# Filler matmuls into an unused PSUM bank in eight waits of TensorE, in a two-layer perceiver kernel on one core

## What is computed

```python
x = x + _L0_xattn_ref(_layernorm(x), ctx_2048, seg, ...)   # 16 heads, latent queries/keys, window of 9 keys a query
x = x + _L0_attn_ref(_layernorm(x), ...)                   # gated state-space mixer, 512 channels, 16 states, a scan
x = x + _L0_ffn_ref(_layernorm(x), ...)                    # 256 -> 1024 -> 256, gelu of a rounded value
x = x + _L1_xattn_ref(_layernorm(x), ctx_2048, ...)        # 16 heads of 16, all 4096 context rows, 8-bit rounding
x = x + _L1_attn_ref(_layernorm(x), ...)                   # self-attention over the pair of batches
x = x + _L1_ffn_ref(_layernorm(x), ...)                    # shared expert and routed expert, 256 -> 1152 -> 256
```

## Time and profile before

| | |
|---|---|
| median of 3 runs | 547.14 us (542.32 to 548.55) |
| the profiled execution | 546.76 us |
| its span, first to last instruction | 544.9 us |
| mean granted TensorE clock, by the page | 0.937 |
| busy: TensorE, VectorE, ScalarE, GpSimd | 80%, 73%, 54%, 25% |

### The profile page before, as it was taken

One profiled execution on the slowest core, in us unless ns is written; L12 is line 12 of the kernel. 1 busy time (PEld: TensorE's weight loads), 2 busy tenths in 40 slices (PEclk: granted clock), 3 DMA queues, 4 the chain that ended last, 5 costly groups with the idle time before them and its releaser, 6 DMA issues.

```text
span 544.9 us, 9508 instructions
## 1 busy us (share of the span) xinstructions
PE 437.3 (80%) x3874; PEld 328.4 (60%) x3914; DVE 398.5 (73%) x607; ACT 296.0 (54%) x384; POOL 138.8 (25%) x176
## 2 busy tenths in 40 slices
PE   3999887788488777767866789899898988876597
PEld 3556776666265555533753567677677767654486
DVE  6134585357969999995669899999999999613242
ACT  2123424045454444431437899999999999931110
POOL 4124441013545555550001233242111111100000
PEclk9999996989699999989889799999999999977789
DMA  8820692131122111004519545544455334000000
GB/s 300 344 91 0 195 246 100 37 158 36 43 95 80 60 58 58 2 0 169 217 47 396 203 159 229 226 165 156 174 228 219 157 156 156 2 1 0 1 1 19
DMA packets 14822, 67.94 MB, mean 125 GB/s; under 512 B 6154, under 2 KB 8762, under 8 KB 11706
## 3 DMA queue, kind: packets, MB, share of 16 engines
q1 hardware_dynamic: 14202, 63.78, 31.8%
q0 software_dynamic: 576, 3.54, 1.7%
HBM read 66.16 MB, written 1.15 MB: 124 GB/s over the span
## 4 chain that ended last, share of the span: by engine, by line
PE 54%; DVE 17%; issue 14%; ACT 8%; DMA 3%; POOL 2%; SPq 1%; DVEq 0%; ACTq 0%; POOLq 0%
PE ps L1705 10%; PE ps L1684 6%; PE ps L1718 4%; PE ps L1793 3%; ACT arena L915 3%; PE ps L1717 3%; DVE arena L1138 3%; DVE arena L1147 3%; PE ps L1375 2%; PE ps L1377 2%; PE ps L1395 2%; DVE arena L1100 2%; PE ps L1505 2%; PE ps L1626 2%; PE ps L1573 2%
## 5 line engine op out<-in xcount | busy, mean ns | idle before, releaser
L1245 DVE CUSTOM_DVE_ANT_0 arena<-ps,arena 128x1024 f32<-128x1024 f32 x88 | 109.1, 1279 | 3.7 <-PE ps L1684 3.6
L1705 PE MATMUL ps<-cst,arena 128*128 128x128 f32 x512 | 78.8, 277 | 18.5 <-ACT arena L915 16.8
L1705 PEld LDWEIGHTS ps<-cst,arena 128*128 128x128 f32 x512 | 61.1, 141 | 50.9 <-ACT arena L906 32.5
L906 ACT ACTIVATE arena<-arena 128x4096 uint8<-128x4096 f32 x22 | 81.7, 3714 | 7.1 <-POOL arena L682 7.0
L1684 PE MATMUL ps<-arena 128*128 128x512 bf16 x216 | 68.5, 383 | 8.0 <-DVE arena L1245 3.4
L1718 PE MATMUL ps<-vrow,arena 128*128 128x16 f16 x1024 | 60.5, 169 | 0.0
L1718 PEld LDWEIGHTS ps<-vrow,arena 128*128 128x128 f16 x1024 | 54.1, 97 | 1.4
L1245 DVE CUSTOM_DVE_ANT_0 w<-ps,arena 128x1024 f32<-128x1024 f32 x40 | 50.0, 1279 | 3.6 <-PE ps L1684 2.7
L915 ACT ACTIVATE arena<-ps 128x512 f32<-128x512 f32 x96 | 50.0, 586 | 1.6 <-PE ps L1718 1.5
L1717 PE MATMUL ps<-vrow,arena 128*128 128x16 f16 x768 | 49.9, 170 | 0.0
L649 POOL TENSOR_TENSOR arena<-arena 128x1024 f32<-128x1024 f32 x16 | 37.5, 2366 | 47.6 <-DVE arena L1138 47.3
(11 more groups left out here) (266 smaller groups left out, 818.3 us busy)
## 6 DMA issues: line engine op xcount, KB each, us to landing
arena<-ks_scr SPq DMA_DIRECT2D x16, 2048.0 KB, 8.1
arena<-in_context SPq DMA_DIRECT2D x16, 512.0 KB, 3.4
arena<-in_w SPq DMA_DIRECT2D x1, 4488.0 KB, 13.5
w<-in_w SPq DMA_DIRECT2D x1, 2927.0 KB, 13.6
arena<-in_w0b SPq DMA_DIRECT2D x1, 2560.0 KB, 11.2
arena<-in_w SPq DMA_DIRECT2D x1, 2048.0 KB, 8.3
arena<-bc_scr SPq DMA_DIRECT2D x16, 128.0 KB, 3.5
arena<-in_fill SPq DMA_DIRECT2D x1, 2048.0 KB, 7.0
```

What stands on the lines that cost most here:

```text
L906: act.activation(out8[:, :, 0], s_sb[u % 3], ACT.Exp, bias=nb[:, u % 3:u % 3 + 1], accum_out=zall[:, u:u + 1]).then_inc(p_ready, 1)
L1245: dve.tensor_tensor_reduce(s_sb[slot][:, keys], ps[:, 2 * (c % 2):2 * (c % 2) + 2, :].rearrange("p a n -> p (a n)"), ksb[h % 2][:, keys], ...
L1705: mm = pe.transpose(bank(4 + n % 3, k * P, P), words[:, w:w + P], ident)
```

## The change

A tile `busy` of 512 bf16 values a partition is set to 1.0 by GpSimd. TensorE multiplies it 28 times into bank 3 before it waits for the first weights. A helper `awake(n)` does n matmuls of the bf16 identity against itself, repeated four times, into bank 3: 12 at the head of `columns(1)` to `columns(5)`, 5 before the transposes of the attention output, 14 before the transposes of the self-attention output. TensorE also waits for the bf16 identity (ScalarE writes it at 4.72 us) ahead of the first weights. Nothing reads bank 3's filler.

```diff
--- before.py
+++ after.py
@@ -143,6 +143,7 @@
         early = vrow.rearrange("k p n -> k (p n)").bitcast(F32)
         csums = early[:, 0:B * CT * D].rearrange("k (b t d) -> k b t d", b=B, t=CT)
         w0q = early[:, B * CT * D:B * CT * D + W0Q]
+        busy = early[:, B * CT * D + W0Q:B * CT * D + W0Q + 256].bitcast(BF16)
         w_dq = w0q[:, 0:CH * QC].rearrange("p (c n) -> p c n", c=CH)
         w_kcat = w0q[:, CH * QC:CH * (QC + 2 * R)].rearrange("p (c n) -> p c n", c=CH)
         w_qr = w0q[:, CH * (QC + 2 * R):W0Q].rearrange("p (h n) -> p h n", h=H)
@@ -324,6 +325,7 @@
         hT = take([FT + 1, T])
         assert at[0] <= 2 * KEYS
 
+        busy_set = sem("busy_set")
         pe_step = sem("pe_step")
         (WABS, QLAT, MTR, MLAT, MLA_OUT, DLAT, DBC, DLIN, MIX_OUT, FF_OUT, Q_PS, Q_TR, ON_TR, X_OUT, Q_MADE,
          KEYS_MADE, VALUES_MADE, OA_TR, SA_OUT, LOGITS) = range(1, 21)
@@ -574,6 +576,7 @@
 
         @block.gpsimd
         def _(pool):
+            pool.memset(busy[:, :], 1.0).then_inc(busy_set, 1)
             pool.memset(neghalf[:, :], -0.5).then_inc(half, 1)
             pool.wait_ge(half, 1)
 
@@ -1327,8 +1330,15 @@
 
         @block.tensor
         def _(pe):
+            def awake(n):
+
+                for _ in range(n):
+                    pe.matmul(bank(3, 0, 512), identb[:, :], identb[:, :].unsqueeze(1).broadcast_to([P, 4, P]), start=True, stop=True)
+
             def columns(k):
 
+                if k:
+                    awake(12)
                 pe.wait_ge(ln_rows, 2 * (k + 1))
                 for c in range(CH):
                     for b in range(B):
@@ -1336,7 +1346,11 @@
                 mm.then_inc(ln_tr, 1)
 
 
+            pe.wait_ge(busy_set, 1)
+            for _ in range(28):
+                pe.matmul(bank(3, 0, 512), busy[:, 0:P], busy[:, :], start=True, stop=True)
             pe.wait_ge(ld_cst, 16)
+            pe.wait_ge(identb_ready, 2)
             pe.wait_ge(ld_w0a, 16)
             for h in range(H):
                 pe.matmul(bank(h // 8, (h % 8) * KVC, KVC, 0, QC), w_uqT[:, h, :], w_ukT[:, h, :], start=True, stop=True)
@@ -1737,6 +1751,7 @@
                 weighted(UNITS - 1, c)
 
 
+            awake(5)
             pe.wait_ge(on_rows, 1)
             for c in range(CH):
                 for b in range(B):
@@ -1764,6 +1779,7 @@
             projected(1, 1, 1).then_inc(pe_step, 1)
             projected(0, 2, 5)
             projected(1, 2, 6).then_inc(pe_step, 1)
+            awake(14)
             pe.wait_ge(oa_rows, B)
             for c in range(CH):
                 for b in range(B):
```

## The result

The changed kernel takes 527.81 us (median of four executions: 523.34, 526.63, 528.98 and 538.56), against 547.8 (four, 542.32 to 548.55). The ratio is 0.963 (0.953 to 0.973). The profiled execution is the one of 523.34 (span 521.5), 23.4 us less than the one profiled before.

What follows compares the result with a forecast made beforehand. TensorE at the lower clock (1.2 of 2.4 GHz) in the first 46 us and behind idle gaps was the bound. Savings 15.7 + 4.45 + 2.25 + 2.6 + 4.1 = 29.1, less 3, give 547.14 - 26.1 = 521.0 us; range 512 to 537.

Steps and rivals of the forecast that it cites:

- start, to the first L1409: From launch through the query rounds: 28 fillers raise the clock early, saving 2.4 + 0.95 + 12.75 - 0.4 = 15.7 us.
- gaps 1, 2, 3: First three layer-norm waits: 12 fillers each keep the clock up for work behind; 4.45 us together, the third trimmed for a transfer.
- five before the attention output: Five fillers in a 1.24 us gap: save 2.25 if they hold the clock, delay by 0.9 if it has fallen.
- gap 4 and the 14: Layer-norm wait and self-attention output: faster matmuls, but filler becomes the late one by 0.5; 2.6 us saved.
- gap 5: Last layer-norm wait: the transposes, L1785 and L1793 behind it run at the high clock; 4.1 us saved.
- allowance for falls: 3 us taken off the sum, since fillers cover only 2.6 of 3.6 to 4.1 us and some gaps fall anyway.
- The reading of the first stretch: First 46 us: the strip's 1.00 is absence of a record; durations show TensorE at the lower clock level.
- They cost 0 to 1.2; I take 0.4: Delay of L1342 by the 28 start fillers, ending at 8.8 to 10.3 us against its start at 9.10.
- Everything to 105.87 hangs on this chain, so it moves along: Work behind the query rounds keeps the start's full 15.7 us; 8 if a transfer of the context were late.
- Rival B: Clock rises but falls back in the first query rounds, 96 rows wide and behind two ScalarE-copy waits: 533.8 us, chance 0.2.
- Rival C: Fillers do not hold: remaining idle drops the clock at every gap, and the start falls back too: 543 us, chance 0.08.
- Rival D: Slower: the clock does not rise on matmuls of one constant bf16 tile, all fillers cost 0.43: 563 us, chance 0.04.

Runs made afterwards that it cites:

- bridged: Changed kernel plus three filler bridges in the start (34 instead of 28 fillers, 6 and 2 more at the ScalarE-copy waits): 522.55 us, ratio 0.958.
- w3b_later: Changed kernel with the load of the last weights (w3b) issued behind the second head's key scales instead of before them: 538.35 us, ratio 0.978.
- the fourth experiment: Same run as w3b_later: changed kernel with the w3b load moved behind the second head's key scales; 538.35 us, ratio 0.978.
- the bridged start: Kernel before plus start fillers only, 34 before the first weights, 6 and 2 at the waits for ScalarE's copies, none in later gaps: 533.97 us, ratio 0.979.
- The version without any low stretch: Changed kernel with bridged start, 16 instead of 12 fillers in layer-norm gaps, and fillers in every other long TensorE wait: 513.9 us, ratio 0.943.

## Why the prediction was right, and where its steps were off

The forecast was 26.1 us less; the medians give 20.0 less, the profiled executions 23.4. The predicted 521.0 is 6.8 us under the measured median; the profiled execution, 523.34, is 2.3 above it, and the executions reach from 520.8 to 540. The forecast was the fast heap of a kernel that has several. Step by step, on the profiled executions (the measured column adds up to 23.4):

| place | predicted | measured |
|---|---|---|
| start, to the first L1409 | 15.7 | 14.5 |
| from there to 105.87 | 0 | -2.5 |
| gaps 1, 2, 3 | 1.6, 1.55, 1.3 | 1.6, 1.5, 1.5 |
| attention loop: behind its tenth product, at its end | 0, 0 | -0.4, -1.1 |
| five before the attention output | 2.25 | 1.4 |
| gap 4 and the 14 | 2.6 | 2.7 |
| gap 5 | 4.1 | 4.1 |
| allowance for falls | -3 | 0 |

The closeness to the profiled execution is in part luck. Without the allowance the sum was 29.1; the 3 were taken off for falls at the gaps, which did not come in this execution, and stood in for other losses: 1.2 in the start, 2.5 behind it, 1.5 in the loop.

*The reading of the first stretch was right*, and it was most of the gain. The page's 1.00 there was no reading: L1389 went from 2.08 to 1.13. The rounds gave 12.5 (from 17.82 to the copy at 36.04 is 18.2, against 30.7), for 12.75 predicted; L1356 came out at the estimated 2.9.

*"They cost 0 to 1.2; I take 0.4" was mis-sized, for a reason that was not the fillers.* L1356 began 1.7 us later than L1342 did, since the weights landed later; the kernels without fillers in the start show the same (10.56, 11.03). A landing time from one profiled execution was taken for a constant. That is the 1.2 missing in the start.

*"Everything to 105.87 hangs on this chain, so it moves along" failed by 2.5.* The chain does move along to 49.38, 14.5 earlier. Then its DMA store takes 3.97 instead of 2.89, and GpSimd's sum 3.43 instead of 2.35: 1.1 each, and L1436 (the old L1422) waits for both. Behind them the clock is low over 66.80 to 80.50, 13.7 us instead of the 10.3 of before, for half a microsecond more. Whether the store and the sum are longer because they now fall into busier stretches was not tried.

*"If the clock has already fallen, they take 2.15 and delay by 0.9" is what happened* at the attention output: the five took 2.29, and delayed L1758 by about 0.7. The case was written down and not chosen. What they gave all the same is L1763 at 1.99 instead of 3.78: a late filler that runs at the lower level can still pay, since the work behind it ran at the higher.

*The transfer was named for gap 3 ("a transfer of scales also holds VectorE") and 0.2 was taken off for it.* Gap 3 brought 1.5 at the first L1248, and the wait for the scales grew from 0.90 to 2.39, but that is not where the loop lost: by the tenth product it was level (13.42 against 13.43). The loop lost its 1.5 elsewhere, and no term had that: *"The attention loop between 306 and 475 is paced by VectorE and gets no filler; I leave it as it is"*. TensorE is on its chain at both ends, and the clock decides how long that takes. At the end the clock falls earlier than before: the reciprocal begins 4.9 to 5.0 us behind the loop's last eviction in the five profiled executions with fillers at the gaps and none in the loop, 3.95 to 3.96 in the four without fillers at the gaps, and 3.96 again in the three with fillers at the loop's end too. Why fillers elsewhere bring that fall about is open.

*"From this I take 3" was about right for some executions, and did not cover the larger risk.* In the execution of 523.34 not one of the five gaps fell, with 1.0 to 1.5 us idle and a copy behind each; in those of 523.57 (bridged) and 539.99 gaps 1 and 2 did, for 3.2 us. The larger risk lay in the start, which I had at full value, and there it is over ten microseconds in single executions and nothing in others. Of eleven executions of the change nine lie from 520.8 to 529.7 and two at 538.6 and 540.0.

*Rival B* had half of the right reason, and a time, 533.8, that no execution of the change took (w3b_later's 533.69 is its slow start and the longer loop together). "Ahead of them are two waits for ScalarE copies" is the cause, as the profile of the fourth experiment and the bridged start show; "the 96-row rounds never raised the clock" is true (27.7 against 46.4) but does not make it fall: in the changed kernel four rounds run without its transposes (L1377), from 17.82 to 26.16, at full rate. A third place, the wait for the first weights, was in no case of mine.

*Rival C* fell as a whole; what it said of the gaps happened at two of five in two profiled executions. The rule beside it, in the Trainium skill, "TensorE: Matmul & The Clock Gate", Part 1, that the ramp costs under 1% of a typical span, doesn't hold for this kernel: the start alone, bridged, is worth 2.1%. The version without any low stretch is 5.7% faster than the kernel before.

*Rival D* fell with the first row: 28 fillers in 8.23 us.

## What to carry to other kernels

Read TensorE's clock from the duration of one repeated instruction, not from the strip, above all ahead of the first record. A filler has to reach from the last work to the next, wait included: half-filled waits give a kernel with heaps 16 us apart, filled ones gave 513.9 with a spread of 1.4, and what reaches beyond the wait costs nearly its full length. Before one books a gain, look for what behind it has a length or a time of its own (a load's landing, a store, a sum on GpSimd). And before one calls a longer wait a loss, look at the next instructions: VectorE's grew by 1.5 us here and the product behind it came on time.

## What was not expected of the hardware

- The clock stayed at the lower level for 26 us of unbroken matmuls, 15.6 of them purely with 96 of 128 rows in use and the rest mixed with 128-row transposes; with all rows, zeros in 32 of them, it rose at 27.7 instead of 46.4 us, at the same instruction durations up to there.
- Work that does not raise the clock can keep it up: the same 96-row rounds ran at the full rate in the changed kernel from 17.82 to 26.16 us.
- In two executions of the same program the clock fell in one behind 2.00 us of waiting (10.88) and not in another behind 1.26 (10.79). The start was 16.4 us longer for it (L1409 at 53.40 against 36.95), of which 13.0 were left at gap 1; the executions took 523.34 and 539.99.
- With twelve fillers and the same 1.53 and 1.03 us of idle behind them, the clock held at gaps 1 and 2 in one execution and fell in two others.
- In the six profiled executions in which TensorE waited for the first weights, with fillers or without, they landed between 9.10 and 11.03 us.
